# Two-layer language model tower: the TTT recurrence with its state update split over four row groups, and two small products moved to GpSimd

## The reference, cut to what matters

```python
def step(carry, inp):
    W1c, b1c = carry                       # [B,H,64,64], [B,H,1,64]
    q, k, v, e = inp
    Z1 = einsum('bhkd,bhde->bhke', k, W1c) + b1c
    grad = ln_l2_bwd(Z1, v - k, ttt_norm_scale, ttt_norm_bias)
    ...                                    # Z1_bar, from q: computed later, from snapshots
    last_e = e[..., -1, :, None]
    W1n = W1c - einsum('bhkd,bhke->bhde', last_e * k, grad)
    b1n = b1c - sum(last_e * grad, axis=-2, keepdims=True)

def ln_l2_bwd(x, target, g, b):
    mu, var = x.mean(-1, keepdims=True), x.var(-1, keepdims=True)
    std = sqrt(var + LN_EPS); xh = (x - mu) / std
    gx = (xh * g + b - target) * g
    return (gx - gx.mean(-1, keepdims=True) - xh * (gx * xh).mean(-1, keepdims=True)) / std
```

## Time and profile before

| | us |
|---|---|
| median of three runs | 1444.83 |
| the profiled execution, its own time | 1442.97 |
| its span | 1441.2 |
| TensorE matmul busy (90% of the span) | 1295.5 |
| VectorE busy (64%) | 919.8 |
| ScalarE busy (49%) | 709.2 |
| GpSimd busy (26%) | 377.0 |
| between 700 and 800 us, TensorE / VectorE / ScalarE / GpSimd busy | 99.3 / 88.0 / 87.9 / 61.7 |

### The profile page before, as it was taken

How to read it: one execution, slowest core, us unless ns; L and a number is a source line. 1 busy time by engine, 2 the same in 40 slices (tenths; PEclk the granted TensorE clock), 3 DMA queues, 4 the chain that set the end, 5 groups by cost and what they waited for, 6 DMA issues and landing times. The chain is left out here.

```text
span 1441.2 us, 29234 instructions
## 1 busy us (share of the span) xinstructions
PE 1295.5 (90%) x11395; PEld 874.1 (61%) x11395; DVE 919.8 (64%) x2227; ACT 709.2 (49%) x1512; POOL 377.0 (26%) x428
## 2 busy tenths in 40 slices
PE   4899999799869999889999998889887788799999
PEld 3432333356537777567777776777664344388888
DVE  6568887423557777499888878887875787500011
ACT  1426555432124443488888874767654233343410
POOL 6400000000047777355666650000000333300000
PEclk9979999869979999899999999999998999999999
DMA  3432121000132334444343452212103100067721
GB/s 94 115 104 61 51 61 30 26 0 1 37 96 90 102 118 133 154 123 126 104 131 101 140 133 60 56 39 61 40 1 131 80 1 0 1 236 289 272 96 45
DMA packets 99285, 127.42 MB, mean 88 GB/s; under 512 B 24589, under 2 KB 87804, under 8 KB 94956
## 3 DMA queue, kind: packets, MB, share of 16 engines
q1 hardware_dynamic: 97612, 123.96, 27.8%
q0 software_dynamic: 1536, 1.59, 0.4%
HBM read 89.06 MB, written 37.88 MB: 88 GB/s over the span
## 5 line engine op out<-in xcount | busy, mean ns | idle before, releaser
L637 DVE TENSOR_REDUCE mx<-bank 128x1 f32<-128x512 f32 x192 | 119.7, 681 | 18.5 <-PE bank L559 18.2
L697 ACT ACTIVATE PT<-bank 128x1024 f32<-128x1024 f32 x96 | 94.3, 1022 | 69.7 <-PE bank L575 69.1
L1729 POOL TENSOR_SCALAR r_grD<-gr 32x192 f32<-32x192 f32 x192 | 101.8, 530 | 101.4 <-DVE gr L1623 56.0
L1460 PE MATMUL bank<-r_grD,ek 128*128 128x256 f32 x384 | 100.9, 399 | 0.0
L2455 DVE TENSOR_TENSOR eo_all<-bank,m_b2s 128x768 f32<-128x768 f32 x8 | 7.7, 958 | 142.3 <-PE bank L2416 142.3
L2447 ACT ACTIVATE x_g<-bank,m_b1s 128x128 f32<-128x128 f32 x192 | 51.4, 400 | 75.7 <-PE bank L2398 75.7
L1460 PEld LDWEIGHTS bank<-r_grD,ek 128*128 128x128 f32 x384 | 68.3, 191 | 9.5
L559 PE MATMUL bank<-K,Q 97*128 97x512 bf16 x192 | 68.9, 411 | 5.1 <-DVE mx L637 3.3
L2331 POOL TENSOR_SCALAR m_xs<-m_xs 128x256 f32<-128x256 f32 x4 | 2.5, 631 | 259.7 <-DVE m_xs L2235 258.6
L1673 ACT ACTIVATE r_t<-r_xh,r_cd 128x64 f32<-128x64 f32 x192 | 70.0, 427 | 0.7
L1451 PEld LDWEIGHTS bank<-gr,r_A 128*128 128x128 f32 x384 | 48.3, 193 | 34.2 <-DVE gr L1623 32.0
(11 more groups left out here) (366 smaller groups left out, 3206.4 us busy)
## 6 DMA issues: line engine op xcount, KB each, us to landing
wb<-in_m_w SPq DMA_DIRECT2D x32, 1152.0 KB, 6.0
k_d<-p_krows SPq DMA_DIRECT2D x48, 256.0 KB, 2.8
ek<-k_d SPq DMA_DIRECT2D x32, 384.0 KB
tgt<-c_d SPq DMA_DIRECT2D x33, 196.0 KB
c_d<-p_rows SPq DMA_DIRECT2D x32, 196.0 KB, 2.9
g_d<-gr SPq DMA_DIRECT2D x32, 192.0 KB
o_G<-g_d SPq DMA_DIRECT2D x32, 192.0 KB, 3.0
qk_d<-a_parts SPq DMA_DIRECT2D x24, 192.0 KB, 3.1
```

What stands on the lines that cost most here:

```text
L637: v.tensor_reduce(mx[u % 2][:, j // 4, j % 4:j % 4 + 1], slot(f"A{u}.{j}"), AX.X, ALU.max).then_inc(*dve.did(f"max{u}.{j}"))
L697: a.activation(PT[kt % 2][:, 2 * hp:2 * hp + 2, :], STB[s % 2][:, :, :], ACT.Exp, scale=DH ** -0.5)\
L1460: last = t_.matmul(SP_[g][:, i * B * E1:(i + 1) * B * E1], ek[r][:, p, :], grD[g][:, i, :, :].rearrange("p b e -> p (b e)"), start=False, ...
L1729: last = g_.tensor_scalar(grD[g][rr, :, b, :], b3(gr[j % RING][rr, cols(g)]), 0.0, None, ALU.bypass)
```

## The change

The state update no longer goes through a block diagonal copy. `into_state` makes twelve matmuls instead of three: for each head pair and batch entry b, the weights are the 32 rows of `ek` that belong to b, the moving operand is the gradient itself (the same 32 rows, 64 columns), and the result goes to a bank of its own for each b. The state of both groups therefore lies in four banks, one for each batch entry, with 240 columns of group 0 and 240 of group 1 in each; ordered batch, pair, channel, then bias. `into_bias` becomes four matmuls of 48 columns. `grD` and its four copies are gone.

Since both groups share the banks, TensorE waits for the state copy of the other group before `into_bias`, and `into_bias` and `into_state` stand directly behind `into_z`. `before` is put ahead of `spread`. The state copy is one ScalarE operation of 960 columns from four banks.

The three operations `t` move from ScalarE to GpSimd, the products `u` and `rl` from VectorE to GpSimd; on VectorE `var` of the other group goes ahead of `red`. Snapshots, their readers and the first state follow the new order of columns; a tile of the output stage is loaded by six DMAs instead of four.

```diff
+        held = lambda g: M["ps8"][:, 0:B, g * SC:(g + 1) * SC]
...
                 def into_bias(g, r):
-                    t_.matmul(SP_[g][:, WC:WC + GC], lastb[:, :], gr[r][:, cols(g)], start=False, stop=False, skip_group_check=True)
+                    for b in range(B):
+                        t_.matmul(held(g)[:, b, GC:SC], lastb[:, :], by_b(gr[r][:, cols(g)])[:, b, :], start=False, stop=False,
+                                  skip_group_check=True)
-                def into_state(g, r, part):
-                    for i, p in list(enumerate(heads(g)))[part]:
-                        last = t_.matmul(SP_[g][:, i * B * E1:(i + 1) * B * E1], ek[r][:, p, :], grD[g][:, i, :, :].rearrange("p b e -> p (b e)"),
-                                         start=False, stop=False, skip_group_check=True)
+                def into_state(g, r):
+                    for i, p in enumerate(heads(g)):
+                        for b in range(B):
+                            rr = slice(32 * b, 32 * b + 32)
+                            last = t_.matmul(held(g)[:, b, i * E1:(i + 1) * E1], ek[r][rr, p, :], gr[r][rr, p * E1:(p + 1) * E1],
+                                             start=False, stop=False, skip_group_check=True)
...
                         into_z(0, r).then_inc(*pe.did(f"Z0.{j}"))
+                        t_.wait_ge(*act.at(f"S1.{j}", sc))
+                        t_.wait_ge(ek_in[r], 16 * (sc * (SPT // RING) + j // RING + 1))
                         into_bias(0, r)
-                        t_.wait_ge(*act.at(f"S1.{j}", sc))
+                        into_state(0, r).then_inc(*pe.did(f"upd0.{j}"))
                         t_.wait_ge(*dve.at(f"xh1.{j}", sc))
                         t_.wait_ge(*ago(pool, "kz1", j, 2, sc))
                         bias(1, sc * SPT + j)
+                        before(1, (j + 1) % KR, sc * SPT + j).then_inc(*pe.did(f"pre1.{j}"))
                         spread(0)
-                        before(1, (j + 1) % KR, sc * SPT + j).then_inc(*pe.did(f"pre1.{j}"))
                         t_.wait_ge(*ago(pool, "kz1", j, 1, sc))
                         gram(0, (j + 1) % KR).then_inc(*pe.did(f"X0.{j}"))
...
# VectorE
-                        v.tensor_tensor(u[g][:, :], xh[g][:, :], g2[:, cols(g)], ALU.mult).then_inc(*mine("u"))
-                        me("u")
+                        if g:
+                            v.wait_ge(*pool.at(f"u1.{j}", sc))
+                        else:
+                            v.wait_ge(*ago(pool, "u0", j, 1, sc))
...
# ScalarE
-                        for i in range(GP):
-                            c = slice(i * E1, (i + 1) * E1)
-                            a.activation(t1[g][:, c], xh[g][:, c], ACT.Identity, bias=cd[g][:, 0, i:i + 1], scale=cd[g][:, 1, i:i + 1])\
-                                .then_inc(*act.did(f"t{g}.{i}.{j}"))
...
-                        a.activation(state_of(to, o)[:, 0:PART], SP_[o][:, 0:PART], ACT.Copy)
...
+                        a.activation(by_b(state_of(to, o)), held(o), ACT.Copy).then_inc(*act.did(f"S{o}.{j}"))
...
# GpSimd
-                            for b in (0, 1, 2):
-                                rr = slice(32 * b, 32 * b + 32)
-                                last = g_.tensor_scalar(grD[g][rr, :, b, :], b3(gr[j % RING][rr, cols(g)]), 0.0, None, ALU.bypass)
-                            last.then_inc(*pool.did(f"d{g}.{j}"))
...
+                            g_.wait_ge(*dve.at(f"cd{g}.{j}", sc))
+                            for i in range(GP):
+                                c = slice(i * E1, (i + 1) * E1)
+                                g_.tensor_scalar(t1[g][:, c], xh[g][:, c], cd[g][:, 1, i:i + 1], cd[g][:, 0, i:i + 1], ALU.mult, ALU.add)\
+                                    .then_inc(*pool.did(f"t{g}.{i}.{j}"))
+                            g_.wait_ge(*dve.at(f"xh{o}.{j}", sc))
+                            g_.tensor_tensor(u[o][:, :], xh[o][:, :], g2[:, cols(o)], ALU.mult).then_inc(*pool.did(f"u{o}.{j}"))
+                            g_.wait_ge(*dve.at(f"rs{o}.{j}", sc))
+                            g_.wait_ge(tgt_in[rn], 16 * turn)
+                            g_.tensor_tensor(rl[o][:, :], rs[o][:, :], tgt[rn][:, HALF + o * GP:HALF + (o + 1) * GP], ALU.mult)\
+                                .then_inc(*pool.did(f"rl{o}.{j}"))
+                            g_.wait_ge(*pool.at(f"rl{o}.{j}", sc))
```

More of the change, by code:

```diff
@@ L1307, in ttt_recur @@
         state_of = lambda s, g: spare[:, g * (WC + GC):(g + 1) * (WC + GC)] if s == 1 or s in range(SPT, STEPS, SPT) else S[g]
-        grD = [sb(f"r_grD{g}", [P, GP, B, E1]) for g in range(G)]
         W0, B0 = M["r_WB"][:, 0, :], M["r_WB"][:, 1, :]
@@ L1324, in ttt_recur @@
         ident, ps, kT_all = M["ident"], M["ps"], M["kT_all"]
-        SP_ = [M["ps2"][g].rearrange("p a n -> p (a n)") for g in range(G)]
+        held = lambda g: M["ps8"][:, 0:B, g * SC:(g + 1) * SC]
         X, Z = [ps[4], ps[7]], ps[5:7]
@@ L1402, in _ @@
                             rr = slice(hh * E1, (hh + 1) * E1)
-                            sp.dma_start(O["Wd"][t][rr, :, rr], M["W_d"][t, rr, :, 0, :]).then_inc(O["tiles_in"][t], 16)
+                            for g in range(G):
+                                sp.dma_start(O["Wd"][t][rr, g * GP:(g + 1) * GP, rr],
+                                             M["W_d"][t, rr, g, 0, :].rearrange("p (h e) -> p h e", e=E1)).then_inc(O["tiles_in"][t], 16)
                             sp.dma_start(O["Gs"][t][:, hh, :], M["g_d"][0, hh, t * P:(t + 1) * P, :]).then_inc(O["tiles_in"][t], 16)
@@ L1419, in prime @@
                 def prime(g):
-                    for i, n in ((0, 2), (2, 1)):
-                        p = g * GP + i
-                        t_.matmul(SP_[g][:, i * B * E1:(i + n) * B * E1].rearrange("p (h b e) -> p h b e", h=n, e=E1), ident[:, :],
-                                  b3(W0[:, p * E1:(p + n) * E1]).unsqueeze(2).to_broadcast([P, n, B, E1]),
-                                  start=True, stop=True, skip_group_check=True)
-                    return t_.matmul(SP_[g][:, WC:WC + GC], ident[:, :], B0[:, cols(g)], start=False, stop=True, skip_group_check=True)
+                    for b in range(B):
+                        t_.matmul(held(g)[:, b, 0:GC], ident[:, :], W0[:, cols(g)], start=(g == 0), stop=True, skip_group_check=True)
+                        last = t_.matmul(held(g)[:, b, GC:SC], ident[:, :], by_b(B0[:, cols(g)])[:, b, :], start=False, stop=True,
+                                         skip_group_check=True)
+                    return last
                 def bias(g, s):
-                    t_.matmul(Z[g][:, 0:GC], ident[:, :], state_of(s, g)[:, WC:WC + GC], start=True, stop=False, skip_group_check=True)
+                    t_.matmul(Z[g][:, 0:GC].rearrange("p (b c) -> p b c", b=B), ident[:, :], by_b(state_of(s, g))[:, :, GC:SC],
+                              start=True, stop=False, skip_group_check=True)
                 def spread(g):
@@ L1599, in half @@
                         v.tensor_tensor(gp[g][:, 1, :], gx_of(g), xh[g][:, :], ALU.mult).then_inc(*mine("pr"))
+                        v.wait_ge(*act.at(f"sq{o}.{j}", sc))
+                        variance(o).then_inc(*others("var"))
                         me("pr")
@@ L1709, in _ @@
                 for r in (2, 3):
-                    g_.memset(KTz[r][:, :, :, :, :], 0.0)
-                for g in range(G):
-                    last = g_.memset(grD[g][:, :, :, :], 0.0)
+                    last = g_.memset(KTz[r][:, :, :, :, :], 0.0)
                 last.then_inc(zeroed, 1)
@@ L1808, in tile @@
                         rr = slice(hh * E1, (hh + 1) * E1)
-                        sp.dma_start(Wd[r][rr, :, rr], M["W_d"][t, rr, :, b, :]).then_inc(tiles_in[r], 16)
+                        for g in range(2):
+                            sp.dma_start(Wd[r][rr, g * PH:(g + 1) * PH, rr], M["W_d"][t, rr, g, b, :].rearrange("p (h e) -> p h e", e=E1))\
+                                .then_inc(tiles_in[r], 16)
                         sp.dma_start(Gs[r][:, hh, :], M["g_d"][b, hh, t * P:(t + 1) * P, :]).then_inc(tiles_in[r], 16)
@@ L1825, in _ @@
                 for r in range(RING):
-                    sp.wait_ge(tiles_in[r], 64 * len(range(r, TILES, RING)))
+                    sp.wait_ge(tiles_in[r], 96 * len(range(r, TILES, RING)))
                 for r in range(2):
```

88 lines of the change are left out of this document (35 added, 53 removed).

## The result

The changed kernel takes 1649.95 us (median of 4 runs, 1644.98 to 1659.96), the kernel before 1444.82 us (4 runs, 1438.65 to 1446.53). The ratio is 1.1448, with a 95% interval of 1.1413 to 1.1482. I had forecast 1453 us and a range of 1442 to 1477: the sign was right, and the loss is 205 us where 8 were forecast.

The account below looks back on a forecast made before the run. A ring through `into_z`, `var`, `t` and the gradient bounds each half, VectorE's own work close beside it. 46 late halves x (4.13 - 3.935) = +9.0, early halves -1.1: 1444.8 + 7.9 = 1453 us, range 1442 to 1477.

Parts of the forecast that it names:

- The step that failed: Reading today's recurrence: 46 halves of 3.935 us at full TensorE clock; no rival priced a lower clock.
- TensorE's sum, 4.06: TensorE's work in one half of the recurrence, without any wait, was to need 4.06 us.
- The new order's two changes of shape: On TensorE, the order `before`, `spread`, `gram` costs two of six tile-shape changes, each 0.095 + 0.11 us.
- The ring, 4.13: Dependent chain of one half, `into_z`, square, `var`, `t`, gradient, back to `into_z`: 4.13 us, from 3.89 to 4.64.
- the gradient's end: Last VectorE gradient operation of a half, taking 0.28 us, ends at 3.96; 0.12 added for GpSimd and VectorE reading together.
- the rival of the lock: Last gradient operation stands 0.6 us behind GpSimd's `u`: half 4.61, +31 us, 1476 us; chance 8%.
- `u` off VectorE brings nothing: The 0.4 to 0.6 us taken from VectorE gain nothing, since `var` waits for the square until 1.30 anyway.
- The state copy hides: ScalarE's state copy, awaited before `into_bias`, is done by 3.8, wanted at 4.06 + 0.66: 0.9 us to spare.
- the rest of the program: Outside the recurrence, snapshots, two more DMAs per output tile, priming and first state were to cost nothing.
- a slow `t`: Rival: GpSimd's `t` takes 0.43 to 0.53 us, period 4.34 to 4.64, time 1462 to 1477 us; chance 16%.

Follow-up runs that it names:

- l1: Changed kernel with `t` back on ScalarE and row sums ahead of the variance, new TensorE order kept, no added spreads: 1647.47 us.
- j2: Changed kernel with `t` back on ScalarE, row sums ahead of the variance, four more spreads in each of the first four halves, new TensorE order kept: 1458.57 us.
- e1: Changed kernel with the held state's loading and twelve filling matmuls moved right ahead of the recurrence loop: 1631.63 us.
- j1: Changed kernel with the old TensorE order and four more spreads in each of the first four halves; `t` stays on GpSimd: 1534.16 us.
- d1: Changed kernel with `t` on ScalarE, old order on TensorE and VectorE, four more spreads in each of the first four halves: 1440.47 us.
- f2: Changed kernel with `spread` issued twice instead of once in each half: 1497.26 us.
- e4: Kernel before with only `u` and `rl` moved from VectorE to GpSimd: 1441.03 us, against 1443.15 us for the kernel before.
- c1: d1 with the bias in two pieces of 96 columns instead of four: 1428.12 us, against 1444.51 us for the kernel before.
- f1: Kernel before with `into_bias` as four matmuls and the order `before`, `spread`, `gram`; dense state update on diagonal copies kept: 1468.54 us.

## Why the prediction was wrong, point by point

**The step that failed** is one that I wrote down as a condition and never priced: halves "at full TensorE clock". The whole sum is in durations at 1.0. It says in so many words that three matmuls of 256 columns go and that loads set the pace of what replaces them, but draws from that only time, nothing for the clock. No rival has a lower clock, which is why the range stops at 1477. What the runs put in its place: TensorE's new work ran at 0.5 from the first half to the last, with halves of 7.29 us. With one spread more in each half and `u` behind the gradient, the same kernel ran at full clock in halves of 4.30 and took 1466.24 us (h1). What the clock is worth by itself, 1647.47 - 1458.57 = 189 us, comes from l1 against j2, a version with `t` on ScalarE; it is most of the 205.

The Trainium skill, "TensorE: Matmul & The Clock Gate", section "Why this matters for your kernels", advises keeping TensorE continuously busy and without long idle gaps, so that it runs at full speed. By that rule the changed kernel would have been safe, and e1 and j1 too, whose gaps are 0.3 to 0.6 us. The traces of this case disagree: 100.00 of 100.00 us busy at 0.50 in the changed kernel, 80.00 of 80.00 at 0.50 in l1. Being busy does not bring this work to the full clock.

**TensorE's sum, 4.06: right.** j2 is bound by TensorE at full clock, with halves of 4.11. The weight loads of one half of j2:

```profile
791.46 0.74 PEld L1455 LDWEIGHTS bank<-gr,r_A 128*128 128x128 f32 x6
792.13 0.97 PEld L1461 LDWEIGHTS bank<-gr,r_lastb 128*128 128x128 f32 x8
793.15 0.76 PEld L1468 LDWEIGHTS bank<-gr,ek 32*128 32x128 f32 x24
793.98 0.30 PEld L1431 LDWEIGHTS bank<-r_S,ident 128*128 128x128 f32 x2
794.50 0.38 PEld L1441 LDWEIGHTS bank<-r_S,KTz 128*32 128x32 f32 x24 [0.23 <-issue]
```

`into_bias` starts at 0.67 (0.66 forecast), `into_state` at 1.69 (1.55 + 0.095), `bias` at 2.52 (2.37 + 0.095), `before` at 3.04 (2.90 + 0.095). The 24 passes of `into_state` take 0.83 to the next load (0.82): the four row groups do go at once. The new order's two changes of shape cost 4.11 - 3.86 = 0.24 to 0.25 (j2 against d1) where I had 2 x 0.205. At full clock TensorE's part would have cost what was forecast of it.

**The ring, 4.13: too short, 4.34.** f2 at full clock gives the times behind the first load at 821.32:

```profile
822.60 0.35 DVE L1564 TENSOR_REDUCE r_var<-r_sq 128x3 f32<-128x192 f32 x1 [0.40 <-ACT r_sq L1645]
...
823.45 0.17 DVE L1618 SCALAR_TENSOR_TENSOR r_cd<-r_sums,r_rl 128x6 f32<-128x6 f32 x1
...
823.78 1.19 POOL L1717 TENSOR_SCALAR r_t<-r_xh,r_cd 128x64 f32<-128x64 f32 x3 [1.46 <-DVE r_rs L1567]
...
824.28 1.32 DVE L1629 SCALAR_TENSOR_TENSOR gr<-o_gate,r_rl,r_t 128x64 f32<-128x64 f32 x3 [0.19 <-POOL r_t L1717]
...
824.94 0.59 POOL L1720 TENSOR_TENSOR r_u<-r_xh,r_g 128x192 f32<-128x192 f32 x1
```

`var` at 1.28 (1.30), `cd` at 2.13 (2.15), `t` from 2.46 to 3.65 (2.42 to 3.63), `u` 0.59 (0.6). One `t` is 0.39 to 0.45, longer than my 0.36, but they follow each other without the gap that I had added. What was mis-sized is the gradient's end: 4.28, where I had 3.96 plus 0.12 for interference. The last operation takes 0.60 beside `u`. This is the rival of the lock, which I gave 8% and priced too high: I let the operation wait for all of `u` and then take its own 0.28. In f2 `u` ends at 4.20, the operation 0.08 after it, and 4.28 + 0.05 = 4.33 is the half. I had argued against it by `pr` beside GpSimd's diagonal copies, which have one input; `u` has two. For `u` the traces agree with the section "Who interferes with whom" on the Trainium skill's page "SBUF — State Buffer" (0.60 beside `u`, 0.27 to 0.36 without). For GpSimd's one-input `t` they don't: the first two gradient operations of f2 run beside it and take 0.34 and 0.29.

**`u` off VectorE brings nothing: right.** In the changed kernel at full clock VectorE waits 0.40 for the square (the first of the lines above). In the kernel before the move alone costs some 6 us (e4). c1, with halves of 3.65, has it too, but no run shows what it is worth there.

**The state copy hides: right.** In f2 it ends 824.95 and `into_bias` wants it at 826.32, 1.37 to spare (0.9 forecast). In the rest of the program nothing of the change stands out: from the last row sums to the end the full-clock runs with the new layout of the state take 585.5 to 591.0 us, the kernel before 585.9 and f1, with the old layout, 591.5.

At full clock the change would thus have cost, by an estimate from f2's half, 46 x (4.34 - 3.935) = 19 us, which is 1464: inside my range, but by the lock and not by a slow `t`, and near h1's 1466.24.

## What to carry to other kernels

Where an edit takes streamed columns off TensorE and leaves weight loads, price the clock as a term of its own: read the granted clock of the stretch first, and give "it drops to 0.5 and stays" a chance and a time. Look at how the loop is entered: in j2 and l1 the same loop ran at 1.0 or at 0.5 for its whole length, after a different first 20 us. Where TensorE's work has been thinned, an idle gap may cost more than its own length (j1, e1), so a wait that looks small (here 0.3 to 0.6 us in each half, for GpSimd's `t`) is worth removing for the clock's sake; the kernel before, with its dense state update, kept its clock with gaps of that size. And when work goes to GpSimd, look at which VectorE operation it will run beside.

## What the runs showed of the hardware that I had not expected

- The granted clock has two lasting states for one loop: 481 us at 0.5, with TensorE busy for all of the 460 us from 600 to 1060 (l1), and 259 us at 1.0 (j2), with the same instructions from the third step on. In f2 it rose by itself after 72 us, in j1 it fell six times.
- More work made the program faster: one added matmul of 384 columns in each half (f2) 1497 us, two (f3) 1482, four (e2) 1486, none 1650. A `spread` costs (4.76 - 4.43) / 2 = 0.165 us.
- VectorE's gradient operation on 64 columns takes some 0.60 us when it starts 0.07 us behind GpSimd's two-input `u` (f2), some 0.50 when `u` is further on (c1), and 0.27 to 0.36 without `u` (h1); if it starts during `u`, it ends 0.08 us after it. Beside GpSimd's one-input `t` it takes 0.28 to 0.34.
